# Expert blocks of 128 rows in pairs, table numbers loaded four at a time, and a finer wait for the split context

## The reference, cut to what matters

```
y = sum over the 8 experts e of  g[e] * (silu(h @ Wgate[e]) * (h @ Wup[e])) @ Wdown[e]      # widths 128 -> 96 -> 128
```

## Time and profile before

| | us |
|---|---|
| median of 3 runs (lowest to highest) | 3863.2 (3858.03 to 3872.15) |
| the profiled execution | 3865.37 |
| its span, first to last instruction | 3863.6 |
| busy: PE, DVE, ACT, POOL | 3139.7, 2202.4, 1664.8, 1411.5 |
| granted TensorE clock, mean | 0.909 of full |

### The profile page before, as it was taken

One profiled execution on the slowest core, in us unless ns is written; L12 is line 12 of the kernel. 1 busy time (PEld: TensorE's weight loads), 2 busy tenths in 40 slices (PEclk: granted clock), 3 DMA queues, 4 the chain that ended last, 5 costly groups with the idle time before them and its releaser, 6 DMA issues. The chain is left out here.

```text
span 3863.6 us, 90063 instructions
## 1 busy us (share of the span) xinstructions
PE 3139.7 (81%) x30574; PEld 2540.3 (66%) x30574; DVE 2202.4 (57%) x5866; ACT 1664.8 (43%) x4673; POOL 1411.5 (37%) x2430
## 2 busy tenths in 40 slices
PE   7999999997742006998799999999987777569998
PEld 5666666666642005887677777777765656459998
DVE  4777676766567303665677776667755556641111
ACT  4666666664520002333244444444435556434443
POOL 1222222222237771000777777777632222220000
PEclk9999999998975558999899999999998998769999
DMA  2000000000021413555111111111100000000000
GB/s 78 22 16 22 18 20 22 16 17 2 0 122 50 131 55 112 150 152 146 35 34 33 33 33 33 33 33 33 30 6 2 0 2 0 1 11 12 11 11 22
DMA packets 158242, 150.49 MB, mean 39 GB/s; under 512 B 18680, under 2 KB 137728, under 8 KB 157696
## 3 DMA queue, kind: packets, MB, share of 16 engines
q1 hardware_dynamic: 141696, 114.86, 9.8%
q0 software_dynamic: 16384, 33.59, 2.9%
HBM read 95.95 MB, written 52.43 MB: 38 GB/s over the span
## 5 line engine op out<-in xcount | busy, mean ns | idle before, releaser
L1656 POOL DMA_INDIRECT y_picked<-f_ys,idy x256 | 246.9, 965 | 394.7 <-POOLq L92 352.5
L1523 ACT ACTIVATE y_prob<-y_ps_s,y_mx 128x514 f32<-128x514 f32 x256 | 176.5, 690 | 445.2 <-DVE y_mx L1731 445.2
L2276 POOL DMA_INDIRECT f_xs<-acc,f_idx x256 | 255.8, 999 | 102.3 <-issue 83.3
L1336 PEld LDWEIGHTS y_ps_o<-y_v,y_pT 128*128 128x128 f32 x2048 | 248.8, 191 | 59.7 <-issue 42.0
L1336 PE MATMUL y_ps_o<-y_v,y_pT 128*128 128x64 f32 x2048 | 272.0, 276 | 11.0 <-DVE y_om L1824 9.7
L77 POOL TENSOR_TENSOR x_px<-x_prob,consts 128x64 f32<-128x64 f32 x256 | 75.9, 296 | 560.2 <-ACT x_prob L856 560.2
L2681 ACT ACTIVATE g_hid<-g_ps_h,g_b 128x512 f32<-128x512 f32 x256 | 176.1, 688 | 240.5 <-PE g_ps_h L100 237.8
L856 ACT ACTIVATE x_prob<-x_ps_s,x_mx 128x289 f32<-128x289 f32 x512 | 250.8, 496 | 45.9 <-DVE x_mx L1017 42.3
L2697 DVE SCALAR_TENSOR_TENSOR x<-g_ps_y,g_w_now,x 128x128 f32<-128x128 f32 x256 | 72.1, 344 | 345.5 <-PE g_ps_y L2647 345.5
L1024 DVE COPY x_pT<-x_ps_t 128x512 f32<-128x512 f32 x256 | 177.1, 692 | 144.3 <-PE x_ps_t L644 140.3
L2472 PE MATMUL fe_ps_x<-consts,fe_xg 128*128 128x128 f32 x384 | 75.5, 278 | 208.7 <-DMA fe_xg<-f_xs 208.6
(11 more groups left out here) (443 smaller groups left out, 8779.3 us busy)
## 6 DMA issues: line engine op xcount, KB each, us to landing
fe_xg<-f_xs SPq DMA_DIRECT2D x192, 128.0 KB, 2.1
f_ys<-fe_yk SPq DMA_DIRECT2D x192, 128.0 KB, 2.1
x_ctxT<-ctx_dram SPq DMA_DIRECT2D x32, 514.0 KB, 3.5
y_ctxT<-ctx_dram SPq DMA_DIRECT2D x32, 514.0 KB, 3.6
f_weights<-w_one_dram SPq DMA_DIRECT2D x1, 10240.0 KB, 28.1
f_xs<-f_zeros SPq DMA_DIRECT2D x64, 128.0 KB, 1.8
f_xs<-acc,f_idx POOLq DMA_INDIRECT x256, 2.2
y_picked<-f_ys,idy POOLq DMA_INDIRECT x256, 2.5
```

Source lines behind the costliest of these rows:

```text
L1336: mm = pe.matmul(ps_o[:, b, at:at + GW], pT[:, u % 2, g, c, :], v[:, b % 2, c, g * D + at:g * D + at + GW], start=(u == 0 and g == 0 and c ...
L1523: ins = act.activation(prob[:, p, :, :], ps_s[:, 2 * p:2 * p + 2, 0:M], ACT.Exp, bias=mx[:, p:p + 1], accum_out=den[:, s, b, p:p + 1])
L1656: pool.indirect_dma_start(out=picked[:, t % 2, k * D:(k + 1) * D], out_offset=None, in_=ys, in_offset=bass.IndirectOffsetOnAxis(ap=idy[:, ...
L2276: pool.indirect_dma_start(out=xs, out_offset=bass.IndirectOffsetOnAxis(ap=idx[:, t, k:k + 1], axis=0), in_=acc[:, t, :], in_offset=None).t ...
```

## The change: what it does, and the diff

- Blocks are 128 rows. There are at most 4096 x 8 / 128 + 64 = 320, worked as 160 pairs; the two halves `c` of a step may now belong to two experts. The region, the table, the constants and the zeros behind each expert follow.
- SP's `load(j)` issues two DMAs of 128 rows, each with its own first row. `load_four` brings four numbers of the table into registers at once, for two pairs. SP has loads alone now, with no step between them.
- On PE, `find(j)` brings the experts of two pairs with `load_four`, behind `up` of the step before; each half's matmuls have their own register.
- The stores are issued by ACT, `store(j-1)` behind `keep_hT(j+1)`. ACT waits for all of them to have landed before it loads its table.
- In the second cross attention, `keys_a` waits for the split of its own batch, at each of the four batches.

```diff
+def load_four(nc, eng, row, at, top):
+    return nc.values_load_multi_w_load_instructions(row[:, at:at + 4], engines=(eng,), min_val=0, max_val=top)[1]
...
             def keys_a(t, s, j):
-                if j == 0:
-                    pe.wait_ge(S["ctx_split"].sem, S["ctx_split"].upto(t))
+                pe.wait_ge(S["ctx_split"].sem, S["ctx_split"].upto(t, j + 1))
...
-REGION = B * N + 2 * P
-BLOCK = 2 * P
-BLOCKS = 192
+REGION = B * N + P
+BLOCK = P
+BLOCKS = 320
+PAIRS = BLOCKS // 2
...
-                sp.dma_start(xs[bass.ds(at, BLOCK), :].rearrange("(c p) d -> p c d", p=P), zeros[:, :, :])\
+                sp.dma_start(xs[bass.ds(at, BLOCK), :], zeros[:, :])\
...
                     if j >= RING:
                         sp.wait_ge(S["xT_turned"].sem, S["xT_turned"].upto(j - RING))
-                    at = sp.value_load(tab[0:1, 0, j:j + 1], min_val=0, max_val=E1 * REGION - BLOCK)
-                    sp.dma_start(xg[:, s, :, :], xs[bass.ds(at, BLOCK), :].rearrange("(c p) d -> p c d", p=P))\
-                        .then_inc(x_in[s].sem, 16)
...
+                    if j % 2 == 0:
+                        at[j], at[j + 1] = (lambda v: (v[0:2], v[2:4]))(
+                            load_four(nc, mybir.EngineType.SP, tab[0:1, 0, :], 2 * j, E1 * REGION - BLOCK))
+                    for c in range(2):
+                        sp.dma_start(xg[:, s, c, :], xs[bass.ds(at[j][c], BLOCK), :]).then_inc(x_in[s].sem, 16)
...
-                for j in range(AHEAD):
+                for j in range(PAIRS):
                     load(j)
-                for j in range(BLOCKS):
-                    if j + AHEAD < BLOCKS:
-                        load(j + AHEAD)
-                    store(j)
...
+                def find(j):
+                    four = load_four(nc, mybir.EngineType.PE, tab[0:1, 1, :], 2 * j, E1 - 1)
+                    expert[j], expert[j + 1] = four[0:2], four[2:4]
...
-                    expert[j] = pe.value_load(tab[0:1, 1, j:j + 1], min_val=0, max_val=E1 - 1)
...
-                                       weights[:, bass.ds(expert[j], 1), 0:2 * F1], start=True, stop=True)
+                                       weights[:, bass.ds(expert[j][c], 1), 0:2 * F1], start=True, stop=True)
...
+                    if j + 3 < PAIRS and (j + 3) % 2 == 0:
+                        find(j + 3)
...
+                def store(j):
+                    s = j % RING
+                    act.wait_ge(S["y_kept"].sem, S["y_kept"].upto(j))
+                    act.dma_start(ys[j * 2 * BLOCK:(j + 1) * 2 * BLOCK, :].rearrange("(c p) d -> p c d", p=P),
+                                  yk[:, s, :, :]).then_inc(y_out[s].sem, 16)
...
+                    if j >= 1:
+                        store(j - 1)
+                store(PAIRS - 1)
+                for s in range(RING):
+                    act.wait_ge(y_out[s].sem, y_out[s].upto(PAIRS // RING - 1))
                 act.preload_act_table_set("natural_log_exp_and_others")
```

More of the change, by code:

```diff
@@ L40 @@
 CONSTS = {"ident": 128, "same8": 128, "head8": 16, "head16": 8, "head8s": 16, "head16q": 4, "quad": 16, "own4": 4, "own4s": 4,
-          "pick": 32, "batch": 4, "iota": 8, "one": 1, "upper": 128, "region": 64, "starts": 16, "blocks": 192}
+          "pick": 32, "batch": 4, "iota": 8, "one": 1, "upper": 128, "region": 64, "starts": 32, "blocks": 320}
 def const_offset(name):
@@ L2172, in route @@
     release(nc, S.values())
-REGION = B * N + 2 * P
-BLOCK = 2 * P
-BLOCKS = 192
+REGION = B * N + P
+BLOCK = P
+BLOCKS = 320
+PAIRS = BLOCKS // 2
+STARTS = B * N // BLOCK
 RING = 8
@@ L2203, in route_one @@
         upper, ones = sb("upper", P, dt=BF), sb("ones", P, dt=BF)
-        cnt, cmp, nb, nb_bf = sb("cnt", 1, p=E), sb("cmp", 16, p=E), sb("nb", 1, p=E), sb("nb_bf", P, dt=BF, p=E)
+        cnt, cmp, nb, nb_bf = sb("cnt", 1, p=E), sb("cmp", STARTS, p=E), sb("nb", 1, p=E), sb("nb_bf", P, dt=BF, p=E)
         shift, vals, tops = sb("shift", E), sb("vals", TILES, E), sb("tops", TILES, 8)
@@ L2207, in route_one @@
         line = sb("line", 4, BLOCKS, p=1)
-        tails, zeros = sb("tails", E, dt=mybir.dt.int32, p=1), sb("zeros", 2, D)
+        tails, zeros = sb("tails", E, dt=mybir.dt.int32, p=1), sb("zeros", D)
         ps = ctx.enter_context(nc.psum_tensor("f_ps", [P, MANY, WIDE], FP32))
@@ L2271, in _ @@
         def _(pool):
-            pool.memset(zeros[:, :, :], 0.0).then_inc(S["zeros"].sem, 1)
+            pool.memset(zeros[:, :], 0.0).then_inc(S["zeros"].sem, 1)
             for t in range(TILES):
@@ L2417, in experts_one @@
         S = signals(nc, "fe", "xT_turned xT up_made silu hid h_turned hT down_made y_kept")
-        x_in = [Signal(nc.alloc_semaphore(name=f"fe_x_in{s}"), 16) for s in range(RING)]
+        x_in = [Signal(nc.alloc_semaphore(name=f"fe_x_in{s}"), 32) for s in range(RING)]
         y_out = [Signal(nc.alloc_semaphore(name=f"fe_y_out{s}"), 16) for s in range(RING)]
@@ L2431, in experts_one @@
             block = inner.enter_context(nc.Block())
-            AHEAD = RING - 1
             def halves(ps, b, w):
@@ L2438, in _ @@
             def _(sp):
+                at = {}
                 def load(j):
@@ L2442, in load @@
                         sp.wait_ge(S["xT_turned"].sem, S["xT_turned"].upto(j - RING))
-                    at = sp.value_load(tab[0:1, 0, j:j + 1], min_val=0, max_val=E1 * REGION - BLOCK)
-                    sp.dma_start(xg[:, s, :, :], xs[bass.ds(at, BLOCK), :].rearrange("(c p) d -> p c d", p=P))\
-                        .then_inc(x_in[s].sem, 16)
[L2447 to L2451, removed]
-                for j in range(AHEAD):
-                    load(j)
-                for j in range(BLOCKS):
-                    if j + AHEAD < BLOCKS:
-                        load(j + AHEAD)
-                    store(j)
-                for s in range(RING):
-                    sp.wait_ge(y_out[s].sem, y_out[s].upto(BLOCKS // RING - 1))
+                    if j % 2 == 0:
[4 more added lines that the diff above has]
+                for j in range(PAIRS):
+                    load(j)
             @block.tensor
@@ L2501, in down @@
                         mm = pe.matmul(ps_y[:, b, c * D:(c + 1) * D], hT[0:F1, b, c * P:(c + 1) * P],
-                                       weights[0:F1, bass.ds(expert[j], 1), 2 * F1:2 * F1 + D], start=True, stop=True)
+                                       weights[0:F1, bass.ds(expert[j][c], 1), 2 * F1:2 * F1 + D], start=True, stop=True)
                     mm.then_inc(S["down_made"].sem, 1)
                 pe.wait_ge(held.sem, held.upto(0))
-                for j in range(-3, BLOCKS):
-                    if j + 3 < BLOCKS:
+                for j in range(-3, PAIRS):
+                    if j + 3 < PAIRS:
                         turn_x(j + 3)
-                    if 0 <= j + 2 < BLOCKS:
+                    if 0 <= j + 2 < PAIRS:
                         up(j + 2)
-                    if 0 <= j + 1 < BLOCKS:
+                    if j + 3 < PAIRS and (j + 3) % 2 == 0:
+                        find(j + 3)
+                    if 0 <= j + 1 < PAIRS:
                         turn_h(j + 1)
@@ L2531, in keep_hT @@
                     act.activation(hT[0:F1, b, :], ps_h[0:F1, b, 0:2 * P], ACT.Copy).then_inc(S["hT"].sem, 1)
-                for j in range(-2, BLOCKS):
-                    if j + 2 < BLOCKS:
+                def store(j):
[3 more added lines that the diff above has]
+                                  yk[:, s, :, :]).then_inc(y_out[s].sem, 16)
+                for j in range(-2, PAIRS):
+                    if j + 2 < PAIRS:
                         silu(j + 2)
-                    if 0 <= j + 1 < BLOCKS:
+                    if 0 <= j + 1 < PAIRS:
                         keep_hT(j + 1)
+                    if j >= 1:
[3 more added lines that the diff above has]
+                    act.wait_ge(y_out[s].sem, y_out[s].upto(PAIRS // RING - 1))
                 act.preload_act_table_set("natural_log_exp_and_others")
@@ L2805, in _constants @@
         "region": np.tile(np.arange(E1) * REGION + 1, (P, 1)),
-        "starts": np.tile(np.arange(16) * BLOCK, (P, 1)),
+        "starts": np.tile(np.arange(STARTS) * BLOCK, (P, 1)),
         "blocks": np.tile(np.arange(BLOCKS), (P, 1)),
```

## The result

The changed kernel takes **3836.0 us** (median of 4 runs, 3830.1 to 3842.5) beside 3865.2 us (3858.0 to 3872.2, 4 runs) for the kernel before on the same chip: a ratio of 0.9925, with a 95% interval of 0.9899 to 0.9952. The profiled execution took 3839.7 us, its span 3837.9.

What follows compares the result with a forecast made beforehand. SP's instruction stream was taken to bound the expert stage: 159 steps of 1.80 us against 335.6 us give -49.4, plus 2.6 at the ends, -46.8 from 3865.4, so 3818 us. Range 3778 to 3864.

Steps and rivals of the forecast that it cites:

- What bounded the kernel: Expert stage before: SP's instruction stream bounds it, not PE or the bytes; 1.64 us a step, 1.757 with long issues and waits.
- The premise that PE waited for rows: Expert stage before: 0.22 us of each step is not PE's, and PE waited for arriving rows 21 times.
- Fewer steps, with the step as it was: Expert stage: 191 intervals become 159, which alone gives 32 x 1.757 = 56 us.
- SP's step of 1.80: SP's queue, expert stage: 3.51 us for two pairs, 1.76 for one, plus 0.04, gives 1.80 us a step.
- I keep 0.04 (ends: 0 and 0.117): SP's queue: long issues and waits, 0.117 us a step before, fall to 0.04 since the store's share leaves.
- PE's step ... I cost it at nothing: PE's sequencer, expert stage: 0.48 us more for two pairs, a step of 1.54 to 1.78, below SP's 1.80; cost 0.
- ACT's store at nothing: ACT, expert stage: 470 + 42 ns a step fits its idle 0.94 us; 0 with SP as bound, 3 us where PE is.
- The ends: +1.3 and +1.3 predicted: Expert stage: +1.3 us for first checks and second issue, +1.3 us for ACT's table load after the last store.
- The finer wait at zero: Second cross attention: PE's 1.34 us before `keys_a` moves to `keys_t`, which awaits DVE's chain; gain 0 (ends: 0 and 36.5 us).
- The rival in which the wait was worth its length: Second cross attention: DVE's chain starts earlier too, up to 36.5 us on top, 3782 us; chance 0.07.
- The sum: Whole kernel: 286.2 against 335.6 us, -49.4, plus 2.6 at the ends, -46.8; forecast 3818 us.
- The other rivals: Expert stage: PE bounds, 3780 us, chance 0.17; four-number read costs partly by register, no change, 0.11; SP's stream longer, 3893 us, 0.07.

Runs made afterwards that it cites:

- SP relieved: The changed kernel, but SP reads no row numbers and loads rows 0 to 511 each time: 3832.4 us, a step of 1.858 us.

## Why the prediction came out as it did

- **What bounded the kernel: right.** SP's stream bound the expert stage: shortening it alone, by the stores, takes the old step from 1.757 to 1.606 us. The premise that PE waited for rows was thin, for these waits were 4.1 us in 200 and those behind TensorE's own sequencer 14.9; that the latter went with SP's stores, to 2.0, is what settles it.
- **Fewer steps, with the step as it was: right.** 32 x 1.757 = 56 us is what the change offers. It got 38.3 back in this stage, because the step grew by 0.113 us, 159 x 0.113 = 18 us.
- **SP's step of 1.80: its build-up right, its long issues mis-sized.** One read and one check for each number, 333 ns an issue for 128 rows: 1.73 us clean, where I had summed 1.76. The failing step is "I keep 0.04 (ends: 0 and 0.117)" for long issues and waits. Waits did go, 0.8 us in 200. The long issues did not leave with the stores: SP's loads themselves take up to 1618 ns and its table reads up to 629. What is above the clean count is 0.14 us in the step, more than the upper end I had given it. Between 1500 and 1700 us, in 107 steps, the issues of over 0.42 us make 8.3 us of it, table reads of over 0.35 us 3.3 and nine pauses of some 0.35 us on the queue 2.7. A tail of 0.14 where I kept 0.04 is 159 x 0.10 = 16 us more than forecast, and the clean count of 1.73 in place of 1.76 is 5 us less: together the 11 us by which 1.870 misses 1.80.
- **"PE's step ... I cost it at nothing": the second failure, and it would have been enough alone.** I bounded it by 1.78 and put it below SP's 1.80. With SP relieved it is 1.858, so that with SP at the forecast 1.80 the step would still have missed by 0.06. My sum spread 0.48 us over two pairs on top of 2 x 1.54 and took gaps of 42 ns. On this queue the gaps are 58, and the whole of `find` stands in one place, 1.52 us in which no matmul is issued. The array has no work queued for the last 0.6: 2 x 1.54 + 0.6 = 3.7 us for two pairs.
- **ACT's store at nothing: right for the changed kernel.** Its issue took 367 ns, not 470, and ran beside `keep_hT`. With the stores still on ACT and no checks on the two queues the step is the array's own 1.538, so the stores cost nothing there either.
- **The ends: +1.3 and +1.3 predicted.** From the start of the scatter's last DMA to the first transposes it was 8.9 us and is 10.1; from the last step's first transposes to the next stage's first gather 8.9 and 10.7. Together +3.0 for 2.6.
- **The finer wait at zero: right**, and for the reason given. VectorE's chain has not moved: from the rotation of the queries to the end of the keys' it is 4.99 us in the tile shown and was 4.95, again without a pause, and `keys_t` waits for it. The rival in which the wait was worth its length (3782 us) is excluded by the ratio of 0.9998.
- **The sum.** -38.3 + 3.0 = -35.3 us in the expert stage and its ends, for -46.8 predicted. The profile shows only 25.7 between the spans, since its first cross attention, whose code is the same but for the width of the constants beside it, took 8.3 us longer than in the profiled execution of before, and the second one 1.4 us longer (the first one's scores, line L635 of the changed kernel):

```profile
L635 PE MATMUL x_ps_s<-x_kT,x_wide x1024: 402/501/846, 26.9 to 900.7; 32*128 32x289 f32 x171
```

The same line in the kernel with the finer wait undone runs from 26.8 to 894.4, in the kernel before from 26.6 to 892.1. Of eleven other profiles none has it over 895.2, so it belongs to that execution. The medians differ by 29 us, and with the finer wait undone by 37; the 35 of the stages lies between. How much of the 29 is such chance of single executions is open.

- **The other rivals.** Steps of 1.54 us came only in every second step; the checks are as many as counted, four to a read. The four-number read costs 27 ns more than a one-number read, as measured on SP. The Trainium skill, "Runtime: NRT & Kernel Launch", section "Instruction fetch mechanics", has about 200 ns for each register, even in bulk; for these reads that does not hold, and the step of 2.10 us estimated by it did not come. The Trainium skill, "DMA: Bandwidth & Descriptors", section "Latency and other measured facts", says that the compiler unrolls such loads four times to spread a floor of about 600 ns. That the cost of a read spreads over four numbers agrees with 300 ns for four; the floor does not.

## What to carry to other kernels

A queue of instructions is an engine too: sum its reads, checks, addresses, issues and gaps for each step, TensorE's queue as well as SP's, and add the tail that the old step shows above its clean count. When two queues come out within a few hundredths of a microsecond of each other, easing one gives next to nothing and easing both gives all that there is down to the next bound: here 0.02 us a step against 0.33. Range checks of numbers that the kernel makes itself are the first thing to leave out: the best version found is the changed kernel without them, 3780.6 us, 2.3% below the kernel before and 55 us below the changed one.

## What was unexpected of the hardware

- A TENSOR_LOAD of four numbers took 300 ns on SP and 332 on TensorE, where TensorE's hardly varied (327 to 334 between 1500 and 1700 us in the changed kernel); one of two numbers 638 and 736 ns on TensorE; one of one number 304, and 478 in a kernel where ACT issued the stores.
- DMA issues of 333 ns were broken by single ones of 0.5 to 1.6 us, 11 of 215 between 1500 and 1700 us. Moving the stores to another queue did not remove them while SP issued two loads a pair without a pause. In the kernel with 256-row loads and nothing else on SP none of the loads took over 0.69 us. What sets them was not tried.
